# Decoder layer on one core: the order of work between the projections and the first expert, changed on all engines

## The reference

```python
q = (x @ W_q.T).reshape(B, S, 8, 64);  k likewise;  v = x @ W_v.T
b = (q * k).sum(-1) / 8
a = -softplus(x @ W_alpha.T + bias).reshape(B, S, 8, 64).sum(-1)
# scan over the tokens, per head: ln = logaddexp(a_t + ln, b_t); the state decays by exp(a_t),
# takes exp(b_t) * v_t, and y = sum over heads of state / exp(ln)
x = layernorm(x + y @ W_o.T)
# 8 experts: relu(x @ in_e.T) @ out_e.T, gate_e = sum of ctx where itok == e
x = layernorm(x + sum_e gate_e * expert_e(x))
x = layernorm(x + ffn(x))                    # three hidden layers of 1024
```

## Time and profile before

| what | value |
|---|---|
| median of three runs | 846.95 us |
| the profiled execution's own time | 850.86 us |
| its span | 849.0 us |
| PE busy | 802.7 us, 95% |
| DVE, ACT, POOL busy | 447.7, 254.8, 223.2 us |
| mean granted clock | 0.975 |

### The profile page before, as it was taken

How to read it: one execution, slowest core, us unless ns; L and a number is a source line. 1 busy time by engine, 2 the same in 40 slices (tenths; PEclk the granted TensorE clock), 3 DMA queues, 4 the chain that set the end, 5 groups by cost and what they waited for, 6 DMA issues and landing times.

```text
span 849.0 us, 12928 instructions
## 1 busy us (share of the span) xinstructions
PE 802.7 (95%) x4342; PEld 691.3 (81%) x4342; DVE 447.7 (53%) x1119; ACT 254.8 (30%) x456; POOL 223.2 (26%) x196
## 2 busy tenths in 40 slices
PE   5999849999999999999999989999999999999995
PEld 4888728888899998999899977888788878887885
DVE  4788657765576757767565634215421542154113
ACT  5677622222322213131312133212221222122110
POOL 2465420000220202020110015332543254325331
PEclk9999869999999999999999989999999999999998
DMA  7700000000312131121311000000000000000000
GB/s 262 247 0 2 0 2 2 1 1 25 100 50 90 61 95 40 44 94 50 100 50 50 1 9 1 1 1 25 0 0 0 25 0 0 0 25 0 1 1 25
DMA packets 16450, 31.45 MB, mean 37 GB/s; under 512 B 1680, under 2 KB 6160, under 8 KB 16400
## 3 DMA queue, kind: packets, MB, share of 16 engines
q1 hardware_dynamic: 16400, 30.82, 11.4%
HBM read 28.72 MB, written 2.10 MB: 36 GB/s over the span
## 4 chain that ended last, share of the span: by engine, by line
PE 50%; issue 25%; POOL 13%; DVE 7%; ACT 2%; DMA 1%; POOLq 1%; DVEq 0%; SPq 0%; ACTq 0%
PE bank L698 22%; PE bank L790 20%; POOL ha_lo L526 8%; PE bank L869 7%; POOL hb_lo L526 4%; DVE x_tok L1043 1%; DVE sp L951 1%; DMA wp_lo_f<-in_wproj 1%; DVE hf L1172 1%; DVE hx_lo L1066 1%; POOL wx_lo_r L487 1%; DVE al L940 1%; DVE vp L933 1%; DVE masked L916 1%; DVE sgn L929 1%
## 5 line engine op out<-in xcount | busy, mean ns | idle before, releaser
L621 ACT ACTIVATE hx_hi<-bank 128x512 fp32r<-128x512 f32 x128 | 76.5, 598 | 266.6 <-PE bank L698 266.4
L790 PE MATMUL bank<-wx_hi,hx_hi 128*128 128x256 f32 x512 | 144.8, 283 | 1.3 <-DVE x_tok L1073 0.9
L790 PE MATMUL bank<-wx_hi,hx_lo 128*128 128x256 f32 x512 | 144.9, 283 | 0.0
L790 PE MATMUL bank<-wx_lo_r,hx_hi 128*128 128x256 f32 x512 | 144.8, 283 | 0.0
L1066 DVE SCALAR_TENSOR_TENSOR hx_lo<-bank,hx_hi 128x512 fp32r<-128x512 f32 x128 | 88.0, 689 | 93.7 <-ACT hx_hi L621 93.6
L526 POOL TENSOR_TENSOR ha_lo<-hf,ha_hi_r 128x512 fp32r<-128x512 f32 x64 | 82.5, 1289 | 114.9 <-DVE ha_hi_r L1179 114.9
L869 PE MATMUL bank<-ha_hi_r,wf_hi_r 128*128 128x512 f32 x256 | 103.7, 405 | 5.8 <-POOL ha_lo L526 5.8
L698 PE MATMUL bank<-xT_hi,wx_hi 128*128 128x512 f32 x256 | 103.2, 403 | 3.3 <-DVE hx_lo L1066 1.7
L790 PEld LDWEIGHTS bank<-wx_hi,hx_hi 128*128 128x128 f32 x512 | 97.8, 191 | 6.0 <-DVE x_tok L1073 1.1
L869 PE MATMUL bank<-ha_lo,wf_hi_r 128*128 128x512 f32 x256 | 102.6, 401 | 0.0
L698 PE MATMUL bank<-xT_lo,wx_hi 128*128 128x512 f32 x256 | 101.5, 396 | 0.0
(11 more groups left out here) (139 smaller groups left out, 1370.1 us busy)
## 6 DMA issues: line engine op xcount, KB each, us to landing
stage<-in_wffn SPq DMA_DIRECT2D x44, 256.0 KB, 2.7
wx_lo_f<-in_wx SPq DMA_DIRECT2D x16, 512.0 KB, 4.9
xs_lo_f<-in_xT SPq DMA_DIRECT2D x4, 512.0 KB, 4.9
x_tok<-in_x SPq DMA_DIRECT2D x1, 2048.0 KB, 10.4
out<-x_tok SPq DMA_DIRECT2D x16, 128.0 KB, 1.7
wp_lo_f<-in_wproj SPq DMA_DIRECT2D x3, 512.0 KB, 6.9
ctx_sb<-in_ctx SPq DMA_DIRECT2D x4, 256.0 KB, 3.2
itok_sb<-in_itok SPq DMA_DIRECT2D x4, 256.0 KB, 4.0
```

What stands on the lines that cost most here:

```text
L621: act.activation(hx_hi[:, place, c], bank[b][:, :], ACT.Relu).then_inc(s_relu_ok, 1)
L790: mm = pe.matmul(bank[2 + j % 2][:, 0:D], x_, w_, start=(c == 0 and i == 0), stop=(c == XC - 1 and i == 2))
```

## The change

The edits, by what they do:

- DVE: `a_sum` (softplus sum) of tile t - 1 is done in tile t, behind `al`, instead of at the end of its own tile. `take_v` of a group is done in its own tiles 2 and 3. The low half of W_o is made in the last tile; the last tile's gates move behind the flag.
- PE: the v products (`values`) come after the second tile of a group instead of the fourth. The output products of tiles 0 to 3 go ahead of the transposes of a_tok and b_tok; tiles 4 to 7 go behind them, then BT, tiles 8 and 9, the extremes and tiles 10 to 15.
- DVE: the residual of group 0 and `norm_means` are done ahead of the branch, on the closed form's c_tok; the slow path loads x again and does them over. Behind the branch only s_ve_ok is raised, and POOL's root follows.
- Expert 0's weights are loaded in group 1's turn of SP's queue. Its high and low halves are made, a quarter at a time, in tiles 0 and 1 of groups 1 and 2, by ACT and POOL.
- POOL: expert 1's low half waits until the four tiles of group 0 are normalised.
- ACT: the copies of u for tiles 0 to 3 come ahead of the two exponentials.

```diff
             for g in range(G):
...
                     sp_.dma_start(x0T[:, b], xT[:, b]).then_inc(s_x0T_in, 16)
+                if g == 1:
+                    load_first(0)
...
             sp_.dma_start(scales[:, :, :], ffn_s).then_inc(s_small_in, 16)
-            for e in range(2):
-                for i, part in enumerate((IN, OUT)):
-                    sp_.dma_start(wx_raw[:, e, part], wx[e, :, part]).then_inc(wx_in[e][i], 16)
+            load_first(1)
...
# POOL
-                    if j < DC and not first:
-                        low_v((g - 1) * DC + j, g - 1, j)
+                    if j >= DC:
+                        low_v(g * DC + j - DC, g, j - DC)
+                    if j < DC and not first and not last:
+                        quarter = (g - 1) * DC + j
+                        pool.wait_ge(s_wxhi_ok, quarter + 1)
+                        a = bass.ds(quarter * (WX // 4), WX // 4)
+                        pool.tensor_tensor(wx_lo[:, 0, a], wx_raw[:, 0, a], wx_hi[:, 0, a].bitcast(F32), ALU.subtract).then_inc(s_wxlo_ok, 1)
...
-            pool.wait_ge(s_A_ok, 1)
-            expert_low(0, 0)
...
             root(0)
+            pool.wait_ge(s_xn_ok, J)
             expert_low(1, 1)
# ACT
-                    if j < DC and not first:
-                        high_v((g - 1) * DC + j, g - 1, j)
+                    if j >= DC:
+                        high_v(g * DC + j - DC, g, j - DC)
+                    if j < DC and not first and not last:
...
+                        act.activation(wx_hi[:, 0, a], wx_raw[:, 0, a], ACT.Copy).then_inc(s_wxhi_ok, 1)
...
+            for t in range(J):
+                act.wait_ge(s_u_mm, t + 1)
+                act.activation(u_sb[:, t], UBANK[t % 4][:, 0:D], ACT.Copy).then_inc(s_u_out, 1)
             act.wait_ge(s_tab_d, 2)
             act.activation(decT[:, :], decT[:, :], ACT.Exp).then_inc(s_tab_exp, 1)
             act.activation(betT[:, :], betT[:, :], ACT.Exp).then_inc(s_tab_exp, 1)
-            high_v(G * DC - 1, G - 1, 1)
-            for t in range(B):
+            for t in range(J, B):
# PE
+            def values(g):
                 pe.wait_ge(s_wp_lo_ok, 4)
+                pe.wait_ge(s_xs_lo_ok, g * J + J)
...
+                    if j == 1:
+                        values(g)
...
+            pe.wait_ge(s_q_out, B + 2)
+            pe.wait_ge(s_k_out, B + 2)
+            pe.wait_ge(s_wo_lo_ok, 1)
+            for t in range(J):
+                output(t)
             pe.wait_ge(s_sp_ok, B + 2)
...
-            for t in range(0, 2 * J):
+            for t in range(J, 2 * J):
                 output(t)
             pe.wait_ge(s_chain, 8)
...
-            for t in range(2 * J, 3 * J):
+            for t in range(2 * J, 2 * J + 2):
                 output(t)
             pe.wait_ge(s_extremes_ok, 1)
...
-            for t in range(3 * J, 4 * J):
+            for t in range(2 * J + 2, 4 * J):
# DVE
                     if j > 0 or not first:
+                        a_sum(t - 1, 1 - r)
                         b_sum(t - 1, 1 - r)
...
+                    if j >= DC:
+                        take_v(g * DC + j - DC, j - DC)
...
+            for e in range(2):
+                gate(B - 1, e, masked[:, e])
+            dve.wait_ge(s_c_ok, 1)
+            dve.wait_ge(s_xtok_in, 16)
+
+            for j in range(J):
+                residual(0, j, s_res_ok, s_bn_ok)
+            norm_means(0, s_bn_ok, s_mv_ok, s_ve_first)
             dve.wait_ge(s_flag_ok, 1)
...
+            dve.wait_ge(s_ve_first, 1)
+            dve.sem_inc(s_ve_ok, 1)
...
-            for j in range(J):
-                residual(0, j)
-            norm_means(0, s_bn_ok, s_mv_ok, s_ve_ok)
             norm_apply(lambda j: group_row(0, j), lambda j: group_row(0, j), 0, s_rstd_ok, s_xn_ok)
```

More of the change, by code:

```diff
@@ L704, in three @@
                 return [(a_hi, b_hi), (a_hi, b_lo), (a_lo, b_hi)]
+            def values(g):
+                pe.wait_ge(s_wp_lo_ok, 4)
+                pe.wait_ge(s_xs_lo_ok, g * J + J)
+                for o in range(DC):
+                    pe.wait_ge(s_v_out, g * DC + o + 1)
+                    a = slice(3 * HD + o * P, 3 * HD + o * P + P)
+                    rows = slice(g * J, g * J + J)
+                    product(bank[6 + o][:, :].rearrange("p (j s) -> p j s", j=J), [pair for c in range(DC) for pair in three(
+                        wp_hi[:, c, a], wp_lo[:, c, a], xs_hi[:, rows, c], xs_lo[:, rows, c])], s_v_mm)
             def project(g):
@@ L717, in project @@
                             (s_a_mm, s_q_mm, s_k_mm)[n])
[L719 to L722, removed]
-                    rows = slice(g * J, g * J + J)
-                    product(bank[6 + o][:, :].rearrange("p (j s) -> p j s", j=J), [pair for c in range(DC) for pair in three(
-                        wp_hi[:, c, a], wp_lo[:, c, a], xs_hi[:, rows, c], xs_lo[:, rows, c])], s_v_mm)
+                    if j == 1:
+                        values(g)
             pe.wait_ge(s_const_ok, 2)
@@ L919, in gate, with a_sum @@
                     accum_out=gates[:, bass.ds(b, 1), bass.ds(e, 1)].rearrange("p b e -> p (b e)"))
+            def a_sum(t, r):
+                dve.wait_ge(s_ln_ok, t + 1)
+                dve.scalar_tensor_tensor(out=sp[:, r], in0=al[:, r], scalar=0.0, in1=sp[:, r], op0=ALU.max,
+                                         op1=ALU.add).then_inc(s_sp_sum, 1)
+                dve.wait_ge(s_sp_sum, t + 1)
+                dve.tensor_reduce(a_tok[:, bass.ds(t, 1)].rearrange("p o h -> p (o h)"), sp[:, r].rearrange("p (h d) -> p h d", h=H),
+                                  AX_X, ALU.add).then_inc(s_sp_ok, 1)
             def b_sum(t, r):
@@ L947, in project @@
                             gate(t, e, masked[:, e])
-                    if j < DC and not first:
-                        take_v((g - 1) * DC + j, j)
-                    dve.wait_ge(s_ln_ok, t + 1)
-                    dve.scalar_tensor_tensor(out=sp[:, r], in0=al[:, r], scalar=0.0, in1=sp[:, r], op0=ALU.max,
-                                             op1=ALU.add).then_inc(s_sp_sum, 1)
-                    dve.wait_ge(s_sp_sum, t + 1)
-                    dve.tensor_reduce(a_tok[:, bass.ds(t, 1)].rearrange("p o h -> p (o h)"), sp[:, r].rearrange("p (h d) -> p h d", h=H),
-                                      AX_X, ALU.add).then_inc(s_sp_ok, 1)
+                    else:
+                        dve.wait_ge(s_wo_hi_ok, 1)
+                        dve.tensor_tensor(wo_lo[:, :, :], wo_raw[:, :, :], wo_hi[:, :, :].bitcast(F32), ALU.subtract).then_inc(s_wo_lo_ok, 1)
@@ new lines, in norm_means, with residual @@
+            def norm_means(n0, stats, means, var):
+                for j in range(J):
+                    dve.wait_ge(stats, n0 + j + 1)
+                    dve.sem_inc(s_bn_tick, 1)
+                    dve.bn_aggr(mv[:, j], bn[:, j]).then_inc(means, 1)
+                dve.wait_ge(means, n0 + J)
+                dve.tensor_scalar(var_eps[:, :], mv[:, :, 1], LN_EPS, None, ALU.add).then_inc(var, 1)
+            def residual(g, j, added, stats):
+                t = g * J + j
+                dve.wait_ge(s_u_out, t + 1 + 4)
+                dve.scalar_tensor_tensor(out=group_row(g, j), in0=u_sb[:, bass.ds(t, 1)].rearrange("p o d -> p (o d)"),
+                                         scalar=c_tok[:, bass.ds(t, 1)], in1=group_row(g, j), op0=ALU.mult, op1=ALU.add).then_inc(added, 1)
+                dve.wait_ge(added, t + 1)
+                dve.sem_inc(s_bn_tick, 1)
+                dve.bn_stats(bn[:, j], group_row(g, j)).then_inc(stats, 1)
@@ L982, in _ @@
             dve.tensor_tensor(decT[:, 1:S], decT[:, 1:S], mT[:, 1:S], ALU.subtract).then_inc(s_tab_d, 1)
-            take_v(G * DC - 1, 1)
-            for e in range(2):
-                gate(B - 1, e, masked[:, e])
             dve.wait_ge(s_tab_exp, 2)
@@ L1019, in _ @@
                 step_path(dve)
+                for j in range(J):
+                    residual(0, j, s_fall_res, s_fall_bn)
+                norm_means(0, s_fall_bn, s_fall_mv, s_fall_ve)
+                dve.wait_ge(s_fall_ve, 1)
                 dve.nop()
@@ L1079, in step @@
                     if front:
-                        residual(g + 1, c)
+                        residual(g + 1, c, s_res_ok, s_bn_ok)
                 if front:
```

55 lines of the change are left out of this document (23 added, 32 removed).

## The result

| | before | changed |
|---|---|---|
| median of 20 runs each | 846.84 us | 840.88 us |
| lowest to highest | 844.21 to 850.21 | 834.13 to 846.03 |
| the profiled execution, its span | 850.86, 849.0 | 837.42, 835.3 |

The ratio is 0.9925, with a 95% interval of 0.9906 to 0.9943: faster by 0.75%, 6.0 us of the medians, where 4.9 were forecast. The two profiled executions differ by 13.4 us (13.7 by their spans), twice as much, so they have to be read by stretches. Views of the changed kernel's profile follow, windows first. Columns: window, its length, busy time (and count) of PE, PEld, DVE, ACT and POOL, granted clock, DMA share, GB/s.

What follows compares the result with a forecast made beforehand. PE bounds the projections; behind them a chain of waits runs to the first expert product at 123.44 us. Norm 3.2 plus an earlier root 1.7 gave 4.9 us, so 842.1 from a median of 846.95; range 839.5 to 845.8.

Steps and rivals of the forecast that it cites:

- The projections: nothing.: PE-bound projection matmuls up to 89.20 us: the change gains 0 there, with no gap among the matmuls.
- The third rival (ACT falls behind): Projections: ACT falls 4 us behind and PE waits 1.3 us at each of eight takings; 852.5 us, chance 0.04.
- The end of the projections.: Last projection to aT: outputs start at 91.6 after 2.0 us idle; aT comes 1.8 or 4.0 us later.
- Both of the cases kept open for the clock: Output products after PE's idle: clock holds (2.9 us for 24 matmuls, aT 95.1) or falls (5.1 us, aT 97.3).
- Tables to flag.: From aT through tables, BT and extremes: flag at 103.1, 104.3 or 105.4 against 106.56; 3.5, 2.3 or 1.2 us earlier.
- The middle case: Clock falls while PE waits for BT: extremes' transposes at 102.7, flag at 104.3, 2.3 us earlier; total gain 4.9 us.
- Branch and residual.: Flag to root: 4.44 us branch and 4.54 residual swap, sum unchanged, gates add 0.58; root 2.9, 1.7 or 0.6 earlier.
- more than the sum: Rival: the branch's 4.44 us shrinks, or the clock rises at once; 8.3 us gained, 838.7 us, chance 0.09.
- Norm.: Group 0's four norm instructions fall from 5.16 to 1.38 us behind POOL's new wait; 3.2 us reach PE.
- The rival that POOL isn't the cause: Norm: the 5.16 us are not POOL's doing, so only 1.7 us remain; 845.2 us, chance 0.05.
- The sum.: Norm's 3.2 plus 2.9, 1.7 or 0.6: 6.1, 4.9 or 3.8 us; middle taken, 842.1 us on the median.

Runs made afterwards that it cites:

- a_again: The changed kernel run again with no edit, as base of the other runs: 840.75 us, 0.9937 of the kernel before; stretch 25.72 us.
- e5: Changed kernel with both transposes ahead of all output products again and ACT's copies of u behind the exponentials: 843.25 us, 0.9958 of the kernel before.
- e9: Kernel before with one memset of 4096 columns between the flag and its load: 852.51 us in a single execution, stretch 38.10 us.
- e8: Kernel before with 60 one-column memsets in DVE's queue, placed where DVE waits for PE ahead of the branch: 844.66 us, 0.9978.
- e1: Changed kernel without POOL's new wait ahead of expert 1's low half: 842.98 us, 0.9961 of the kernel before.
- e3: Kernel before with one line added, POOL's wait for the four normalised tiles ahead of expert 1's low half: 842.29 us, 0.9966.
- e2: Changed kernel with group 0's residual and norm_means behind the branch again, gates unmoved: 842.63 us, 0.9959 of the kernel before.
- e7: Changed kernel with output waits, W_o's low half, last gates, POOL's root and six increments moved: 835.9 us, 0.9846 of before; again 830.89, 0.9835.
- e4: Kernel before with 24 empty instructions ahead of the branch, dropped at build, so the kernel before once more: 845.63 us, 0.9973.

## Why the prediction was right, step by step

- **The projections: nothing.** Held; PE 68.00 of 68.00 us busy from 12 to 80, and 7.00 of 7.00 to 87. The third rival (ACT falls behind) has no trace.
- **The end of the projections.** "PE starts the output products at 91.6, 2 us behind its last projection": 3.06 us. The step was mis-sized by 1.0 us, all of it in DVE: `take_v` of tile 14 ended 1.0 us before PE's end (86.09 of 87.07), where I had 87.6 of 89.6. I had summed DVE's instructions at their undisturbed times; beside expert 0's quarter `sp` took 1.80 us instead of 0.68 (61.88, above), and where it didn't, the lead was 1.3 us longer. The length of tile 15's `a_sum` was off as well, 1.51 us instead of 0.69; I had not asked what POOL does beside it. Both of the cases kept open for the clock occurred: it fell in the first profile (aT 7.64 us behind PE's end, forecast 7.7) and held in a_again (6.31, forecast 5.5). That 7.64 meets 7.7 is luck: the outputs started 1.0 us later than forecast and took 4.26 us instead of 5.1, since the clock was back after 3 us and not after 5.9. The 2.4 and 1.2 GHz of the forecast stand in no trace; what the traces show is a granted clock of 1.00 and 0.50, and beside them 0.12 and 0.21 us a matmul of the output products.
- **Tables to flag.** Forecast 13.5 (clock held), 14.7 (it falls while PE waits for BT) or 15.8 us (it falls ahead of the outputs) behind the projections' end; measured 13.97 with the clock held and 15.30 with it fallen ahead of the outputs. The middle case, on which the forecast stands, occurred in neither profile: from BT to the extremes the 12 matmuls stood 0.12 us apart in both. What the four tiles in front of the transposes did was sized by e5 (1.5 us); the halved work between BT and the extremes was not tested by itself.
- **Branch and residual.** "The 4.44 us ... and the 4.54 ... change places; both stay in DVE's own order, so their sum stays." This step failed. The sum went from 8.98 to 7.32 us (102.37 to 109.69), though it now holds the gates, for which the forecast added 0.58: 2.2 us less than forecast. The gap itself fell from 4.44 to 2.0. The rival "more than the sum" had half of the gap going, at a chance of 0.09, but for the wrong reason: not the flag's age in memory (e9: 4.53), but the place of the branch (e8: 2.19). By the stretch that rival's 8.3 us came nearer than the forecast: a_again has 8.1.
- **Norm.** Forecast 3.2, measured 3.5 by the trace, and 2.2 to 2.9 by the medians of e1 and e3. The rival that POOL isn't the cause falls.
- **The sum.** The prediction's own sums are 6.1 us with the clock held, 4.9 for the middle case and 3.8 with it fallen ahead of the outputs. The stretch fell by 8.1 with the clock held and by 6.8 with it fallen there, so like against like 2.0 and 3.0 us were missing. The branch is 2.2 of each and the norm 0.3; the flag came 0.5 later than its case in the first and 0.5 earlier in the second. The medians moved by 6.0, with an interval of 4.8 to 8.0 us. That the forecast of 842.1 lies so near 840.88 is in part luck: it rests on a case that no profile shows and leaves out the 2.2 us of the branch, and the median moved by less than the stretch of either profile. Why it did, the runs don't settle.

The traces show VectorE and GpSimd lengthening each other's instructions, in both orders (`sp` and expert 0's quarter, above) and in three more places: `sp` 1.51 us instead of 0.68 beside qk, a gate 1.37 instead of 0.34 and a residual 1.50 instead of 0.47 beside expert 0's quarters. Not every instruction is lengthened: all 16 `b_tok` sums of the changed kernel take 0.67 to 0.69 us, the one at 58.71 too, which lies inside the quarter from 58.55 to 59.84. I had priced POOL's work for the norm of group 0 and not for DVE's `a_sum` in the projections and behind them, where `sp` took 1.1 and 0.8 us longer.

## What to carry to other kernels

Ask of every VectorE instruction on the path what GpSimd does beside it (`sp`, a gate and a residual took 0.8 to 1.1 us longer each here, the `b_tok` sum nothing); one wait in GpSimd's queue gave 3.5 us, and behind the first product e3, which has it, took no longer than e8, which doesn't (721.1 us each). A branch on a value from memory costs 1.3 to 4.5 us here, 2.2 of it set by where it stands in the program (4.44 in the kernel before, 2.19 in e8), so put the work that does not need it ahead of it, and whatever another engine can do (the root) under it. Wherever the tensor engine runs out of work for 3 us, read two profiles before pricing the clock (it was 0.50 in one and 1.00 in the other here), and split the stretch by markers from that engine's own last instruction, since absolute times move between executions (the projections of the changed kernel ended at 87.07 and at 88.59).

## What the hardware showed that I had not expected

- The gap of load and branch is 4.44, 4.47, 4.14 and 4.53 us (before, e3, e2, e9), and 2.19 with 60 small instructions more in front of it (e8); in the changed kernel it is 2.0 from `var_eps` to the root, and 1.34 in e7.
- A VectorE `sp` that starts 0.03 us behind a GpSimd instruction takes 1.80 us, one that starts 0.02 us ahead 0.68, with GpSimd's growing from 1.28 to 1.81; which comes first differed between two runs of one program, and so did 1.3 us or more of VectorE's lead on TensorE.
- The granted clock after 3.06 to 3.07 us of idle PE was 0.50 in the changed kernel's first profile and 1.00 in its second; the code and the work ahead were the same. The outputs then took 0.21 us a matmul for 3 us, or 0.12 at once.
- The same kernel's span behind the first expert product differs by 1.4 us (721.2 and 722.6, changed) or 3.5 (725.6 and 722.1, before and e4), with the granted clock from 480 to 520 at 1.00, 0.96, 0.91 and 0.96 in this order.
